# A transformer block with gated attention and eight experts: order and banks of the transposes, banks of the value chunks, and the place of VectorE's loop turn

## The reference, cut to what matters

```
h = layernorm(x) * (1 + ca) + sa
q, k, v = h @ W_Q, h @ W_K, h @ W_V            # 16 heads of 64
scores = (q . k) / 8, keys after the row set to -1e6
probs = softmax(scores); z = probs @ v
x = x + ga * (z @ W_out + b_out)
h = layernorm(x) * (1 + cb) + sb
w = softmax over the two largest of h @ Wr + br
x = x + gb * sum_e w[e] * (gelu(h @ W1[e] + b1[e]) @ W2[e] + b2[e])
```

## Time and profile before

| | |
|---|---|
| median of three executions | 1926.4 us |
| the profiled execution's own time | 1924.18 us |
| its span, first to last instruction | 1922.4 us |
| PE busy | 1887.2 us, 98% |
| DVE busy | 1650.9 us, 86% |
| ACT busy | 1541.4 us, 80% |
| POOL busy | 729.1 us, 38% |
| granted TensorE clock, mean | 1.000 |

### The profile page before, as it was taken

The page is one execution under the profiler, slowest core; times in us unless marked ns, Lnnn a source line. Parts: engine busy times, 40 slices in busy tenths (PEclk is TensorE's granted clock), DMA queues, the critical chain, the costliest instruction groups (busy, mean ns, idle before and its releaser), DMA issues.

```text
span 1922.4 us, 50930 instructions
## 1 busy us (share of the span) xinstructions
PE 1887.2 (98%) x15326; PEld 1424.8 (74%) x15326; DVE 1650.9 (86%) x4388; ACT 1541.4 (80%) x3664; POOL 729.1 (38%) x1212
## 2 busy tenths in 40 slices
PE   8999999999999999999999999999999999999999
PEld 6676766767767767667677776888888888888887
DVE  7888888888888888888888888999988889899998
ACT  7888888888888888888888888877777777777775
POOL 4454444444444444444444443222222222222221
PEclk9999999999999999999999999999999999999999
DMA  4100000000000000000000002111111111111111
GB/s 130 57 2 1 0 1 1 0 1 1 0 1 1 0 1 1 1 1 0 1 1 0 1 2 72 62 50 49 49 49 55 49 49 49 49 49 49 49 50 56
DMA packets 42622, 50.04 MB, mean 26 GB/s; under 512 B 3160, under 2 KB 24464, under 8 KB 42512
## 3 DMA queue, kind: packets, MB, share of 16 engines
q1 hardware_dynamic: 42256, 48.41, 8.0%
q0 software_dynamic: 256, 0.53, 0.1%
HBM read 44.47 MB, written 4.46 MB: 25 GB/s over the span
## 4 chain that ended last, share of the span: by engine, by line
PE 70%; issue 12%; ACT 12%; DVE 6%; DVEq 1%; ACTq 0%; DMA 0%
PE banks L589 9%; ACT probs L927 8%; PE banks L561 7%; PE banks L663 6%; PE banks L665 6%; PE banks L664 6%; PE banks L682 6%; PE banks L684 6%; PE banks L683 6%; PE banks L576 4%; PE banks L513 3%; DVE probs_T L1200 3%; PE banks L515 3%; PE banks L514 3%; ACT k_hi L912 2%
## 5 line engine op out<-in xcount | busy, mean ns | idle before, releaser
L491 POOL TENSOR_SCALAR probs<-probs,rdenom 128x512 f32<-128x512 f32 (+3 forms) x1024 | 523.6, 533 | 630.9 <-DVE rdenom L1216 630.9
L927 ACT ACTIVATE probs<-probs,neg_max 128x512 f32<-128x512 f32 (+3 forms) x1024 | 565.0, 552 | 100.2 <-DVE neg_max L1207 100.2
L1032 ACT ACTIVATE hidden<-banks,b_cols 128x512 f32<-128x512 f32 x512 | 349.6, 688 | 177.7 <-PE banks L665 177.3
L1207 DVE CUSTOM_DVE_ANT_0 probs<-banks,mask_w 128x512 f32<-128x512 f32 (+3 forms) x1024 | 434.0, 480 | 3.4 <-issue 2.2
L1383 DVE TENSOR_TENSOR hid_lo<-hidden,hid_hi 128x512 fp32r<-128x512 f32 x512 | 380.0, 753 | 56.5 <-ACT hid_hi L1040 42.4
L477 POOL TENSOR_TENSOR acc<-acc,y_w 128x512 f32<-128x512 f32 x110 | 152.1, 1382 | 461.6 <-DVE y_w L1396 459.8
L589 PE MATMUL banks<-probs_T,v_sb 128*64 128x512 f32 (+3 forms) x2048 | 303.9, 439 | 0.0
L1200 DVE COPY probs_T<-banks 128x1024 f32<-128x1024 f32 (+1 forms) x256 | 232.4, 949 | 25.3 <-PE banks L576 25.2
L589 PEld LDWEIGHTS banks<-probs_T,v_sb 128*64 128x64 f32 x2048 | 136.0, 136 | 155.0 <-issue 118.4
L561 PE MATMUL banks<-k_hi,q_hi 64*128 64x512 f32 (+3 forms) x1024 | 187.7, 360 | 24.7 <-DVE attn_T L1230 10.0
L663 PE MATMUL banks<-h_hi,w_hi 128*128 128x512 f32 x512 | 205.8, 402 | 0.2 <-issue 0.2
(11 more groups left out here) (178 smaller groups left out, 3417.9 us busy)
## 6 DMA issues: line engine op xcount, KB each, us to landing
w_rows<-w_kept SPq DMA_DIRECT2D x128, 256.0 KB, 4.4
x_all<-in_L_attn_resid_dram SPq DMA_DIRECT2D x16, 256.0 KB, 2.8
w_raw<-in_L_ffn_W_dram SPq DMA_DIRECT2D x16, 256.0 KB, 5.2
out_dram<-y_result SPq DMA_DIRECT2D x15, 256.0 KB, 2.3
v_sb<-in_L_attn_W_V_dram SPq DMA_DIRECT2D x1, 512.0 KB, 5.4
hidden<-in_L_attn_W_out_dram POOLq DMA_DIRECT2D x2, 256.0 KB, 5.8
v_sb<-in_L_attn_W_Q_dram SPq DMA_DIRECT2D x1, 448.0 KB, 3.7
v_sb<-in_L_attn_W_K_dram SPq DMA_DIRECT2D x1, 448.0 KB, 4.4
```

What stands on the lines that cost most here:

```text
L491: pool.tensor_scalar(part, part, rdenom[:, p % 2, 4 * h + r:4 * h + r + 1], 1.0, ALU.mult, ALU.mult)\
L927: act.activation(part, part, ACT.Exp, bias=neg_max[:, p % 2, col:col + 1], scale=-1.0, accum_out=denom[:, p % 2, col:col + 1]).then_inc(p_ ...
L1032: act.activation(hidden[:, e % 2, c, :], banks[:, c, :], ACT.Gelu, bias=b1_cols[:, e * HC + c:e * HC + c + 1]).then_inc(hid, 1)
L1207: dve.tensor_tensor_reduce(out=probs[:, p % 2, h, at:at + n], in0=S_BANK[u][h][:, col:col + n], in1=mask_w[:, 512 - n:512], scale=-SCALE, ...
```

## The change

It has five parts.

1. The order of the transposed units becomes 2, 0, 1, in exchanged banks: unit 2 goes to banks 4 and 5, unit 0 to banks 6 and 7, unit 1 stays in 0 and 1. `T_PLACE` gives each unit's place for those who wait. One wait for all eight rows of POOL stands before the first group; the two others are gone. DVE copies unit 2 first and unit 0 second. ACT does its last exponential of a pair before its copy of unit 1 instead of after it.
2. A value chunk that is alone in its pair goes to bank 3 instead of 6, except at p = 4 and 5 (`chunk_banks`). The next pair's score unit 0 waits until ACT has copied it.
3. DVE's loop turns in the middle of pair 6 (the seventh) instead of pair 2. ACT's stays.
4. For DVE the cut between `front` and `rear` moves up to behind the six masking steps, so that the statistics, the rests and the rest of the old `front` stand behind the turn.
5. `ln_apply` and `norm_rows` at p = 3 and 4 move ahead of `rest_z`, `rest_q` and `rest_k`.

Behind the attention loop the last pair's transposes are put in the same new order, in the banks that `T_PAIR_END` names.

```diff
+def chunk_banks(p, first, last):
+
+    n = len(chunks(p, first, last))
+    return [1] if n == 1 and p not in (4, 5) else [i % 2 for i in range(n)]
...
-        T_PAIR, T_PAIR_END = [4, 0, 6], [6, 4, 0]
+        T_PAIR, T_PAIR_END = [6, 0, 4], [0, 4, 6]
+        T_PLACE = [2, 3, 1]
...
                     def transposes(b, p, u, first_bank):
 
-                        wait_alone(pe, p_norm, pair(8, b, p) + (4, 8, 8)[u])
...
-                            if p > 0 and len(chunks(p - 1, first, last)) > 1:
+                            put = chunk_banks(p, first, last)
+                            if p > 0 and 1 in chunk_banks(p - 1, first, last):
                                 pe.wait_ge(v_done, 8 * b + chunks(p - 1, first, last)[-1] + 1)
+                            if p == 0 and not first:
+                                pe.wait_ge(v_done, 8 * b + 1)
...
-                                values(b, p, n % 2, i)
+                                values(b, p, put[n], i)
...
                                 pe.wait_ge(s_masked, done + 6)
+                                wait_alone(pe, p_norm, pair(8, *prev) + 8)
+                                transposes(*prev, 2, T_PAIR[2])
+                                if 0 in put:
+                                    pe.wait_ge(v_done, 8 * b + now[len(put) - 1 - put[::-1].index(0)] + 1)
+                                wait_alone(pe, s_masked, done + 8)
                                 transposes(*prev, 0, T_PAIR[0])
                                 if not young:
                                     pe.wait_ge(z_done, pair(1, *prev))
                                 if has_next:
                                     pe.wait_ge(q_lo, pair(1, *nxt) + 1)
+                                pe.nop(nofuse=True)
                                 transposes(*prev, 1, T_PAIR[1])
-                                pe.wait_ge(s_masked, done + 8)
-                                if now:
-                                    pe.wait_ge(v_done, 8 * b + now[(len(now) - 1) // 2 * 2] + 1)
-                                transposes(*prev, 2, T_PAIR[2])
...
+                    wait_alone(pe, p_norm, pair(8, end, NP))
+                    transposes(end, NP - 1, 2, T_PAIR_END[2])
+                    wait_alone(pe, hid, 2)
                     transposes(end, NP - 1, 0, T_PAIR_END[0])
-                    pe.wait_ge(z_done, pair(1, end, NP - 1))
+                    wait_alone(pe, z_done, pair(1, end, NP - 1))
                     transposes(end, NP - 1, 1, T_PAIR_END[1])
-                    pe.wait_ge(hid, 2)
-                    transposes(end, NP - 1, 2, T_PAIR_END[2])
...
+                        exponentials(b, p, 1, 2)
                         if not begin:
                             evac_T(*prev, first and p == 1)
-                        exponentials(b, p, 1, 2)
...
                         mask_and_max(b, p, 1, 2)
+
+                    def rear(b, p, first, last):
...
                         if p == 2 and not last:
                             ln_stats(b + 1)
...
+                        if p in (3, 4) and last:
+                            norm_rows(0, (2 * p - 6, 2 * p - 5))
+                        if p in (3, 4) and not last:
+                            ln_apply(b + 1, (2 * p - 6, 2 * p - 5))
                         if not early:
                             rest_z(*two_before(b, p))
                         if has_next and not begin:
                             rest_q(*nxt)
                             rest_k(*nxt)
-                        if p in (3, 4) and last:
-                            norm_rows(0, (2 * p - 6, 2 * p - 5))
-                        if p in (3, 4) and not last:
-                            ln_apply(b + 1, (2 * p - 6, 2 * p - 5))
...
-                    def rear(b, p, first, last):
-                        begin, prev = first and p == 0, before(b, p)
                         if p == 2 and not first:
                             gate_attention(b - 1)
                         if p == 4 and not first:
                             add_attention(b - 1)
                         if not begin:
+                            evac_T(*prev, 2, first and p == 1, T_PAIR[2])
                             evac_T(*prev, 0, first and p == 1, T_PAIR[0])
-                            evac_T(*prev, 2, first and p == 1, T_PAIR[2])
-
-                    batches_from_middle(dve, front, rear)
+
+                    batches_from_middle(dve, front, rear, 6)
```

More of the change, by code:

```diff
@@ L111, in batches, with batches_from_middle @@
             body(B - 1, False, True)
-        def batches_from_middle(engine, front, rear):
-            middle = 2
+        def batches_from_middle(engine, front, rear, middle):
             def upto(b, first, last):
@@ L914, in evac_T @@
                     def evac_T(b, p, begin, first_bank=T_PAIR[1]):
-                        act.wait_ge(t_ps, pair(3, b, p) + 2)
+                        act.wait_ge(t_ps, pair(3, b, p) + T_PLACE[1])
                         if not begin:
@@ L1070, in front @@
                             round_w(1, 1)
+                        put = chunk_banks(p, first, last)
                         if now:
-                            values_out(b, 0, now[0])
+                            values_out(b, put[0], now[0])
                         exponentials(b, p, 0, 2)
@@ L1078, in rear @@
                         now = chunks(p, first, last)
-                        for n, i in enumerate(now[1:]):
-                            values_out(b, (n + 1) % 2, i)
+                        put = chunk_banks(p, first, last)
+                        for n, i in zip(put[1:], now[1:]):
+                            values_out(b, n, i)
                         if p == 5 and not last:
@@ L1196, in evac_T @@
                     def evac_T(b, p, u, begin, first_bank):
-                        dve.wait_ge(t_ps, pair(3, b, p) + u + 1)
+                        dve.wait_ge(t_ps, pair(3, b, p) + T_PLACE[u])
                         if not begin:
@@ L1408, in front @@
                     def front(b, p, first, last):
-                        begin = first and p == 0
-                        early = first and p < 2
-                        prev, nxt = before(b, p), after(b, p)
-                        has_next = not (last and p == NP - 1)
+                        begin, nxt = first and p == 0, after(b, p)
                         mask_and_max(b, p, 0, 0)
@@ L1415, in front @@
                         if not begin:
-                            invert_sums(*prev)
+                            invert_sums(*before(b, p))
                         mask_and_max(b, p, 0, 1)
@@ L1423, in front @@
                         mask_and_max(b, p, 1, 2)
+                    def rear(b, p, first, last):
+                        begin, early = first and p == 0, first and p < 2
+                        prev, nxt = before(b, p), after(b, p)
+                        has_next = not (last and p == NP - 1)
                         if p == 2 and not last:
```

4 lines of the change are left out of this document (2 added, 2 removed).

## The result

The kernel after takes 1895.49 us (1895.46 to 1896.85, four runs) against 1926.34 for the kernel before on the same chip: ratio 0.9841 [0.9824, 0.9858]. It is faster by 30.9 us (27 to 34 by the interval) where 6.8 were forecast, and the time lies outside the forecast's range of 1904 to 1930. The profiled execution's span is 1893.7 us against 1922.4.

What follows compares the result with a forecast made beforehand. PE, busy 98% of the span, was taken as the bound, so only its gaps and waits could move the time. Terms: 12 x 0.73 - 3 x 0.46 - 0.6 = 6.8 us, 1926.4 to 1919.6; range 1904 to 1930.

Steps and rivals of the forecast that it cites:

- The turn leaves p=2: From p=2's transposes to p=3's scores: DVE's loop turn no longer delays `attn_T`, 2.45 becomes 1.28, gain 1.17 us per loop batch.
- The 0.38 in the body of p=3: From p=3's scores to its transposes: 7.81 would become 7.43 without the stall, but DVE-POOL port contention was expected to cancel it.
- each waits for the other: At p=3 and 4, `xn` and POOL's rows block each other: POOL ends at M + 6.30 instead of 5.66 (M: DVE's first mask).
- the 0.64 charged to each: Delay of p=3's and p=4's transposes by two `xn` beside POOL's rows: M + 6.51 against M + 5.87 (M: first mask).
- Rival A: POOL and DVE don't hinder each other at p=3 and 4: 12.0 us more gain, 1907.6; chance 0.25.
- The turn arrives at p=6: DVE's 2.69 us turn is hidden by 0.90 of waiting for ACT and p=6's 12 extra products; p=7's mask stays X + 1.46.
- Third key chunk first: New transpose order, all eight POOL rows awaited: gains 0.35 at p=5, about 0.1 at p=2; costs 0.59 at p=7, 0.21 at p=1.
- The lone chunk in bank 3: ACT copies it during the transposes, so cost taken as nothing; uncovered, score unit 0 would wait up to 0.2.
- Into p=5: From p=4's transposes to p=5's scores: `ln_apply` out of `add_attention`'s way and earlier copies make 1.72 become 1.28, gain 0.44.
- PE's turn: PE's loop turn stays in place; 0 to 0.3 might return with 16 instead of 8 transposes behind its last wait; taken as 0.
- The batches without a stall: Three later batches without the stall of DVE's turn: each forecast to lose 0.46 us.
- Rivals B and C: B: turn at p=6 costs over 2.69, 1926.8 at 0.6 more, chance 0.18. C: POOL becomes the pace, 1934.0, chance 0.15.

Runs made afterwards that it cites:

- 2, 1, 0: Kernel after with the transposed units in this order at p=4 and 5 only (second head ahead of the first): 1892.60 us, ratio 0.9826.

## Why the prediction was wrong

**The turn leaves p=2:** right to 0.01 (1.17 against 1.16), from the straight batch's rows. The 0.38 in the body of p=3 would come "too, but see the port below"; it did, 0.46.

**The step that failed most, "each waits for the other"** in the part on `ln_apply`. It rested on one row of POOL that took 1.00 beside a DVE operation with two inputs from SBUF, and `xn` has one. The other direction is right: `xn` waits, 0.45 us per pair of them. POOL's rows are 4.10 in the kernel after with and without two `xn` beside them, and 523.6 us in all in the kernel before with and without the part. Nor is POOL what p=3 and p=4 wait for last: its rows end 0.30 to 0.44 before the weight loads start, so that even the 0.64 charged to each would have been hidden in part. The forecast put -0.43 on p=3 and 4, the trace has +0.58: 1.0 of the 1.75 us by which a loop batch was wrong, or 12 of the 21 us in the 12 loop batches (24 in all). Rival A named this mechanism and its sign ("at 4.08, A is right"); its 1907.6 still lacked 12 us of gain, for the reasons below. That the second input is what holds POOL up is what the adds of the expert stage show (1.48 to 1.71 instead of 1.29).

**The Trainium skill's rule** (page "SBUF — State Buffer", section "Who interferes with whom"), by which whichever engine starts first shuts the other out, held for `xn` in one direction only: DVE 1.04 instead of 0.59, POOL 533 ns a row with and without.

**The turn arrives at p=6:** that it is hidden was right, its price was not. M was put at X + 1.46 and is X + 1.10, because the turn there shows 0.5 to 0.8 beyond the wait for ACT instead of 1.8, and DVE's copies wait for PE again. With that, and with a release of 0.07 for the 0.21 that had been read from one row, the charge on p=7 is 0.15, not 0.59: 12 x 0.44 = 5.3 us. That "the twelve turns are alike" was true of p=2 only; the same turn shows 0 to 2.7 by its place, and nine of the twelve were about 2.5. The cut, which the working used without pricing it, is worth 20.6 us at p=6.

**Third key chunk first:** p=1 is 8.18 from T to T against 8.25 forecast, p=2 0.16 against 0.1, and p=5 0.42 against 0.25. The lone chunk in bank 3, taken as nothing, costs nothing as the change has it; that 0.5 twice a batch hangs on the new bank was not seen.

**Into p=5,** 0.44 was forecast and 0.17 came. The second group, now 8 transposes behind the first, waits for the chunk's copy in bank 6. The two experiments on it agree: `ln_apply` alone brings the full 0.43 in the old order, and 2, 1, 0 brings the rest of it back in the new.

**PE's turn,** "between 0 and 0.3 might come back", taken as 0: 0.35 came, which in the 13 batches ahead of which PE turns its loop is 4.6 us. (X of p=0 is T + 1.60 in batches 2 to 14 of the kernel before and T + 1.28 in 1 and 15, which PE reaches without a turn.) The reason given (16 instead of 8 transposes behind the last wait) is refuted by the run with the new order undone, where 8 stand behind it and X is T + 1.28. The banks alone bring 0.2 of it, but their body of p=0 grows by as much; the two runs that move only DVE's turn bring 0.1 (T + 1.50). How these add up to the 0.35 stays open.

**The batches without a stall** were forecast at -0.46 and gained 0.8 to 0.9. The same terms fail in them: the charge on p=3 and 4, and PE's turn in the first of the two.

**Rivals B and C** did not occur: M of p=7 is X + 1.10, and the release is under 0.1.

## What to carry to other kernels

Price a contention from the pair of operations that will meet, in the direction that will occur, and ask which of the two has slack: here DVE alone waited, inside a wait it had anyway. Put a loop's turn behind the last thing that others wait for and ahead of a wait of the engine's own, and read the instruction queue's packets before and after, for the same turn stalls its engine 2.4 us or not at all (which pays only where the stall was not hidden: p=4 and 5 gained nothing over p=6). Parts of a change that look idle by themselves (a bank, a buffer) can carry another: undo each in the full change as well as trying it alone (the banks were worth 0 and 15 us).

## What the runs showed of the hardware that was not expected

A loop's turn is dear only where it fetches: 60 packets and 0.49 MB more for 12 turns, on DVE (turn at p=2, 3 and 6) and on ACT (at p=4), and no idle without them (DVE at p=4 and 5, ACT at p=2). Of the five packets of a turn DVE waits for one alone, 1.9 to 2.4 us from its start, and part of that can lie under work still in flight or under a wait for ACT: 2.7 us show at p=2 and 0.5 at p=6. What decides whether a turn fetches is open. As the loop's length hardly changes with the pair it turns in, it should be where the loop's code begins; no run moved the code alone, so this was only argued.

DVE and POOL hold each other up by the kind of DVE's operation. An `xn` (one input from SBUF) that starts during a POOL operation lasts until 0.08 us after it, and POOL loses nothing. A `hid_lo` (both inputs from SBUF) lasts until 0.55 to 0.65 after POOL's add, and if it was there first the add is 0.2 to 0.4 longer; a `y_result` (one input from SBUF, one from PSUM) that was there first costs the add nothing (1.29 to 1.30).
